# Queries turned ahead of a wait and copied out of PSUM by ScalarE instead of VectorE, in a four-layer kernel

## The chip, the cores and the metric

The kernel runs on one core of a Trainium2 chip. The metric is the device time of one execution in microseconds; the number compared is the median of several executions. Five engines take part, each with its own queue of instructions worked off in order, and they meet only in semaphores: TensorE (PE; matrix products and transposes into PSUM), VectorE (DVE), ScalarE (ACT), GpSimd (POOL) and SyncE (SP, which issues the transfers here). PEld is TensorE's weight load. PSUM holds eight banks of 512 f32 per partition.

## The reference, cut to what matters

Four residual layers are applied in turn to x of 8 x 16 x 16 x 64 f32, each on a group norm of x: a convolution, a memory layer, a local attention and a two-dimensional scan. The change lies in the end of the memory layer:

```python
q = _l2norm(jnp.einsum('btcd,de->btce', x, Wq))
def step(carry, x_t):          # 16 steps: one gradient step on each image's own weights
    ...
    new_mom = jax.tree.map(upd_m, mom, g)
    new_params = jax.tree.map(upd_p, params, new_mom)
(paramsT, momT), _ = jax.lax.scan(step, (params0, mom0), jnp.swapaxes(x, 0, 1))
final = jax.tree.map(lambda p: jnp.mean(p, axis=0), paramsT)
return _mlp(final, q)          # for w1, w2 in params: h = h + gelu(h @ w1) @ w2
```

Each of the 8 images has its own four matrices, called w10, w20 (first block of the small network) and w11, w21 (second block) in the kernel. After the 16 steps they are averaged over the images, and the averaged network is applied to the normalised queries q. The queries depend on x alone and not on the 16 steps.

## The kernel before

All of x stays on the chip. Each engine has its own program, written out by hand in one order; no planner moves anything. The memory layer projects keys, gates and queries, and GpSimd writes the normalised queries, positions in rows, into the buffer hf (L339, semaphore `q_spread`) before the loop of 16 steps (`Fori`) begins. The loop body spreads over four engines. The last things a step does are: TensorE's outer products for the gradients (helper line L1110), w10's last (semaphore `g10`); GpSimd's decayed copies of the weights (L350, L359, semaphores `kept_...`); and VectorE's updates, which add the momentum in PSUM banks 0 to 3 to the decayed copy. These are w10 (L754), w20, w11 and, at the head of the next step or behind the loop, w21 (all three at helper line L747). Each update sets the semaphore of its matrix (`w10_new` and so on), which reaches 17 with the last one.

Behind the loop the programs stand like this:

- TensorE waits for the last w10 and sums w10 over the images into bank 6 (`mean_of_images`, L1185, semaphore `wm_tp`). Then it waits for `q_spread`, turns the eight 128x128 blocks of hf into banks 4 and 5 (L1194, semaphore `q_tp` once, at the end), and waits for `wm_ready`, `qt_ready` and the last w11, w20 and w21. Then come the first up projection (`up`, L1204), the mean of w11 (L1185 again), and the down projection (`down`, L1211).
- ScalarE waits for `wm_tp`, evicts the mean as w10m (L514, `wm_ready`), and then applies gelu to the four banks of the up projection (L518).
- VectorE does the three remaining updates, waits for `q_tp`, copies both banks of turned queries at once into qt (L801, `qt_ready`), and then sums w20 and w21 over the images (L804 to L809, `wm_sum`), which the down projections take as weights. Later it adds qt to the first block's output (L811).
- GpSimd has nothing to do there until the layer's end.

Before the turned queries, banks 4 and 5 hold scratch of a step. Its last readers are ScalarE's and VectorE's operations that the last gradients wait for.

Of the kernel before, what the change touches and what calls it, by code (L numbers as in the profile page):

```python
# [10 lines left out]
ACT = mybir.ActivationFunctionType  # L11
# [4 lines left out]
BH, J = 2, 4  # L16
HW = H * W
POS = J * HW
NT = 2 * POS
P = 128  # L20
# [6 lines left out]
BANK = 512  # L27
# [50 lines left out]
def conv_attn_scan_kernel(nc, xs_d, band_d, const_d, param_d, out_d):  # L78
    ctx = ExitStack()
    with ctx:  # L80
        def sb(name, shape):
            return ctx.enter_context(nc.sbuf_tensor(name, shape, F32))
# [3 lines left out]
        def sem(name):  # L86
            if name not in sems:
                sems[name] = ctx.enter_context(nc.semaphore(name))
            return sems[name]

        ps = ctx.enter_context(nc.psum_tensor("ps", [P, 8, BANK], F32))
        psf = ps[:, :, :].rearrange("p b n -> p (b n)")
# [4 lines left out]
        def cst(name, rows=P):  # L97
            a, b = CONST_COLS[name]
            return const[0:rows, a:b]

        def par(name):
            a, b = PARAM_COLS[name]
            return param[:, a:b]

        ident = cst("ident")
# [51 lines left out]
        qt = sb("qt", [P, POS])  # L157
# [47 lines left out]
        hf = sb("hf", [P, POS])  # L205
# [204 lines left out]
        def _(act):  # L410
# [99 lines left out]
                               ACT.Copy).then_inc(sem("x_now"), 1)  # L510


            act.wait_ge(sem("wm_tp"), 1)
            act.activation(w10m[:, :], ps[:, 6, 0:E1], ACT.Copy, scale=1.0 / B).then_inc(sem("wm_ready"), 1)  # L514
            for i in range(2):
# [92 lines left out]
        def _(dve):  # L608
# [134 lines left out]
            def updated(m, new, grad, count):  # L743

                dve.wait_ge(sem(grad), count)
                dve.wait_ge(sem("kept_" + new), count)
                dve.tensor_tensor(by_pair(w11 if m == 1 else we[:, m, :]), momentum(m), by_pair(qe[:, m, :]), ALU.add)\  # L747
                   .then_inc(sem(new), 1)
# [47 lines left out]
                updated(1, "w11_new", "g11", t + 1)  # L796

            updated(2, "w21_new", "g21", NS + 1)

            dve.wait_ge(sem("q_tp"), 1)  # L800
            dve.tensor_copy(qt[:, :], psf[:, 4 * BANK:6 * BANK]).then_inc(sem("qt_ready"), 1)  # L801

            dve.wait_ge(sem("w20_new"), NS + 1)
            link(dve.tensor_reduce(wms[:, 0, :], we[:, 0, :].rearrange("p (b d) -> p d b", b=8), AX_X, ALU.add))  # L804
# [158 lines left out]
        def _(pe):  # L963
# [18 lines left out]
            for q in range(2):  # L982
                mm = pe.matmul(ps[:, 1, :], inv512[:, :], sq[:, q, :], start=(q == 0), stop=(q == 1))
# [14 lines left out]
            for d in range(3):  # L998
                pe.matmul(ps[:, 1, :], bandv[96:128, d, 2, :], xpad[96:128, 0, :, d:d + C], start=(d == 0), stop=False)
                mm = pe.matmul(ps[:, 0, :], bandv[0:32, d, 2, :], xpad[0:32, 1, :, d:d + C], start=False, stop=(d == 2))  # L1000
# [4 lines left out]
            for m in range(2):  # L1005
                mm = pe.matmul(ps[:, 2, 0:2], cst("sum16"), csum[:, :, m], start=(m == 0), stop=(m == 1))
# [4 lines left out]
            for q in range(2):  # L1011
                pe.wait_ge(sem("x1_rows"), q + 1)
                for j in range(J):
                    col = 2 * BANK + j * HW + q * P
                    mm = pe.transpose(psf[:, col:col + P], xs[:, q, j * P:(j + 1) * P], ident)
# [25 lines left out]
            for hh in range(2):  # L1041
                for j in range(J):
                    if hh == 0:
                        pe.wait_ge(sem("xn_ready"), j + 1)
                    at = (hh * J + j) * 2 * P
                    mm = pe.matmul(psf[:, at:at + P + 6], xn[:, j * HW + hh * P:j * HW + hh * P + P], keys_gates, start=True, stop=True)
                mm.then_inc(sem("kg_done"), 1)
            for hh in range(2):
                for j in range(J):
                    mm = pe.matmul(ps[:, 4 + hh, j * P:(j + 1) * P], xn[:, j * HW + hh * P:j * HW + hh * P + P], par("wq"), start=True, stop=True)  # L1050
# [18 lines left out]
            for bank in range(J):  # L1069
                mm = pe.matmul(ps[:, bank, :], zero_bf[:, 0:P], zero_bf[:, :], start=True, stop=True)  # L1070
# [6 lines left out]
            with pe.Fori(0, NS) as t:  # L1077
# [21 lines left out]
                def turn(bank, col, x):  # L1099
                    return pe.transpose(ps[:, bank, col:col + P], x, ident)  # L1100
# [47 lines left out]
                for n, x in enumerate((act_u[:, 0, :], h1bd, rbd, k_now)):  # L1148
                    mm = turn(7, n * P, x[:, :])
# [15 lines left out]
                for j in range(J):  # L1165
                    mm = pe.matmul(ps[32 * j:32 * j + 32, 5, 3 * P:4 * P], dhbd[:, 32 * j:32 * j + 32], wd[:, 0, P * j:P * j + P],  # L1166
                                   start=True, stop=True)
# [10 lines left out]
                gradient(3, k_lr, dz0_tok).then_inc(sem("g10"), 1)  # L1178


            pe.wait_ge(sem("w10_new"), NS + 1)

            def mean_of_images(w):
# [3 lines left out]

            mean_of_images(w10).then_inc(sem("wm_tp"), 1)

            pe.wait_ge(sem("q_spread"), 1)  # L1190
            for hh in range(2):
                for j in range(J):
                    at = 4 * BANK + j * HW + hh * P
                    mm = pe.transpose(psf[:, at:at + P], hf[:, (hh * J + j) * P:(hh * J + j + 1) * P], ident)  # L1194
            mm.then_inc(sem("q_tp"), 1)
            pe.wait_ge(sem("wm_ready"), 1)
            pe.wait_ge(sem("qt_ready"), 1)

            def up(w, src, i):
                for n in range(4):  # L1200
# [36 lines left out]
            for n in range(NK):  # L1237
# [3 lines left out]
                for half in range(2):  # L1241
                    for i in range(J):
                        mm = pe.matmul(psf[32 * i:32 * i + 32, 2 * BANK + n * P:2 * BANK + (n + 1) * P],
                                       cst("head_sum")[:, 32 * half:32 * half + 32], prod[n % 4][:, (2 * i + half) * P:(2 * i + half + 1) * P],
                                       start=(half == 0), stop=(half == 1))
                mm.then_inc(sem("qk_sum"), 1)

            def turn_probs(slot, src):
                return pe.transpose(psf[:, 6 * BANK + slot * P:6 * BANK + (slot + 1) * P], src, ident)

            keep_warm(6, 7)
            for half, (first, end) in enumerate(EXP_PARTS):
                pe.wait_ge(sem("exp_done"), half + 1)
                for n in range(first, min(end, 8)):
                    mm = turn_probs(n, ex[:, n * P:(n + 1) * P])
# [199 lines left out]
```

## Time and profile before

| what | value |
|---|---|
| time, median of 3 runs | 324.86 us (324.80 to 325.09) |
| the profiled execution's own time | 322.84 us |
| its span, first to last instruction | 321.0 us |
| mean granted TensorE clock | 0.979 |
| TensorE busy | 280.7 us, 87% |
| VectorE busy | 212.1 us, 66% |
| GpSimd busy | 145.6 us, 45% |
| ScalarE busy | 144.6 us, 45% |

The profile is one execution, recorded by the hardware. Times in rows are microseconds from the start of the span, unless marked ns. A row of the timeline merges neighbouring instructions of one engine and line; in brackets stands how long the engine idled before it and what it waited for. The chain of waits is followed back from the last instruction to what released it each time; "issue" in it is time in which the engine waited for nothing that the profile shows. The loop of 16 steps lies between about 51 and 213 us, each step taking about 10.05 us; the attention and the scan follow behind about 234 us.

### The profile page before, as it was taken

The page shows a single profiled execution, that of the slowest core. Times are in us where ns is not written, and L with a number is a line of the kernel's source. Part 1 is how long each engine was busy: PE and PEld are TensorE (multiplying, and loading weights), DVE is VectorE, ACT ScalarE, POOL GpSimd, SP SyncE. Part 2 cuts the span into 40 slices and gives each one's busy share as a digit, 9 for nine tenths or more (in the row PEclk, how much of TensorE's full clock was granted, in tenths as well). Part 3 has the DMA queues.
Part 4 walks back from the last instruction along what each step waited for, and adds up shares of the span by engine and source line. Part 5 has one row for each costly group of instructions (what it writes and reads, how often), then busy time and mean ns, then how long its engine had stood idle before and what let it go on. Part 6 is the DMA issues. An engine that isn't in the chain of part 4 may idle for free.

```text
span 321.0 us, 8491 instructions
## 1 busy us (share of the span) xinstructions
PE 280.7 (87%) x3338; PEld 186.9 (58%) x3345; DVE 212.1 (66%) x392; ACT 144.6 (45%) x353; POOL 145.6 (45%) x227
## 2 busy tenths in 40 slices
PE   8698759999999999999999999979985774899992
PEld 3233545777777777777777777754333552446642
DVE  0827554656666566665666656675478699899995
ACT  2003554466454664546655466523311662078511
POOL 8300087776667766677666776650000067200000
PEclk9999977999999999999999999999999998999998
DMA  7000000000000000000000000000000000000001
GB/s 289 14 0 2 0 1 2 0 0 0 0 0 0 0 0 0 0 0 0 0 0 0 0 0 0 0 2 2 0 0 2 0 2 0 1 2 0 0 0 65
DMA packets 874, 3.09 MB, mean 10 GB/s; under 512 B 96, under 2 KB 96, under 8 KB 864
## 3 DMA queue, kind: packets, MB, share of 16 engines
q1 hardware_dynamic: 864, 2.96, 2.5%
q8 instruction: 6, 0.10, 0.1%
q14 instruction: 4, 0.03, 0.0%
HBM read 2.44 MB, written 0.52 MB: 9 GB/s over the span
## 4 chain that ended last, share of the span: by engine, by line
PE 68%; DVE 23%; ACT 3%; issue 3%; POOL 2%; DVEq 0%; POOLq 0%
PE ps L1100 16%; PE ps L1082 9%; PE ps L1091 9%; PE ps L1110 6%; DVE arena_mem L754 4%; PE ps L1287 3%; PE ps L968 3%; PE ps L1318 2%; DVE arena_att L830 2%; PE ps L1166 2%; PE ps L993 2%; PE ps L1211 2%; DVE uf L850 1%; PE ps L1326 1%; ACT act_u L471 1%
## 5 line engine op out<-in xcount | busy, mean ns | idle before, releaser
L968 PE MATMUL ps<-zero 128*128 128x512 bf16 x130 | 34.7, 412 | 5.2 <-DVE uf L850 2.9
L350 POOL TENSOR_TENSOR arena_mem<-arena_mem,keep_e 128x512 f32<-128x512 f32 x32 | 33.4, 1043 | 0.0
L359 POOL TENSOR_TENSOR arena_mem<-arena_mem,keep_d 128x512 f32<-128x512 f32 x32 | 33.3, 1040 | 0.0
L747 DVE TENSOR_TENSOR arena_mem<-ps,arena_mem 128x512 f32<-128x512 f32 x49 | 32.0, 681 | 0.0
L481 ACT ACTIVATE arena_mem<-ps 128x512 f32<-128x512 f32 x48 | 28.7, 597 | 7.1 <-PE ps L1100 5.0
L1100 PE MATMUL ps<-const_sb,arena_mem 128*128 128x128 f32 x192 | 31.5, 287 | 0.0
L968 PEld LDWEIGHTS ps<-zero 128*128 128x128 bf16 x137 | 13.6, 106 | 24.6 <-issue 9.2
L471 ACT ACTIVATE act_u<-ps 128x128 f32<-128x128 f32 x32 | 8.9, 277 | 38.1 <-PE ps L1082 38.1
L366 POOL TENSOR_SCALAR z_e<-z_sq 128x128 f32<-128x128 f32 x32 | 9.5, 298 | 33.4 <-ACT z_sq L472 33.3
L1091 PE MATMUL ps<-act_u,arena_mem 128*64 128x16 f32 x512 | 20.6, 211 | 2.3
L1091 PEld LDWEIGHTS ps<-act_u,arena_mem 128*64 128x64 f32 x512 | 18.0, 137 | 7.7 <-issue 6.6
L765 DVE TENSOR_TENSOR ps<-ps,eta_d 128x512 f32<-128x512 f32 x32 | 22.1, 691 | 0.0
L765 DVE TENSOR_TENSOR ps<-ps,eta_e 128x512 f32<-128x512 f32 x32 | 22.1, 691 | 0.0
L1100 PEld LDWEIGHTS ps<-const_sb,arena_mem 128*128 128x128 f32 x192 | 20.1, 140 | 1.5
L770 DVE SCALAR_TENSOR_TENSOR z_y<-z_sq,ps 128x128 f32<-128x128 f32 x32 | 9.2, 288 | 16.9 <-ACT z_sq L472 16.3
L754 DVE TENSOR_TENSOR arena_mem<-ps,arena_mem 128x512 f32<-128x512 f32 x16 | 11.1, 692 | 13.2 <-PE ps L1110 13.2
L1110 PE MATMUL ps<-arena_mem 32*128 32x128 f32 x512 | 18.8, 283 | 0.2
L399 POOL TENSOR_TENSOR arena_att<-arena_att 128x1024 f32<-128x1024 f32 x2 | 5.5, 2761 | 28.7 <-DVE arena_att L850 28.6
L1110 PEld LDWEIGHTS ps<-arena_mem 32*128 32x128 f32 x512 | 15.8, 186 | 4.4 <-issue 4.4
L499 ACT ACTIVATE arena_mem<-ps,lrn 128x512 f32<-128x512 f32 x16 | 11.0, 687 | 10.8 <-PE ps L1100 10.8
L369 POOL TENSOR_TENSOR z_f<-z_e,act_u 128x128 f32<-128x128 f32 x32 | 14.6, 456 | 2.7
L791 DVE SCALAR_TENSOR_TENSOR arena_mem<-arena_mem,ps 128x128 f32<-128x128 f32 x16 | 4.6, 288 | 16.3 <-PE ps L1166 16.3
(267 smaller groups left out, 634.0 us busy)
## 6 DMA issues: line engine op xcount, KB each, us to landing
param_sb<-param SPq DMA_DIRECT2D x1, 840.5 KB, 7.2
arena_conv<-band SPq DMA_DIRECT2D x1, 576.0 KB, 5.6
xs_sb<-xs SPq DMA_DIRECT2D x1, 512.0 KB, 3.2
out<-xh SPq DMA_DIRECT2D x2, 256.0 KB, 2.1
const_sb<-const SPq DMA_DIRECT2D x1, 449.5 KB, 4.1
```

The costliest lines, as they stand in the source:

```text
L350: pool.tensor_tensor(qe[:, m, :].rearrange("p (b d) -> p b d", b=8), we[:, m, :].rearrange("p (b d) -> p b d", b=8), keep_e[:, bass.ts(t, ...
L359: pool.tensor_tensor(by_pair(kept), by_pair(w), keep_d[:, bass.ts(t, J)].unsqueeze(2).broadcast_to([P, J, E1]), ALU.mult).then_inc(sem("ke ...
L369: pool.tensor_tensor(z_f[:, i, :], z_e[:, i, :], act_u[:, i, :], ALU.mult).then_inc(sem("pool_link"), 1)
L481: act.activation(we[:, 1, :] if m == 1 else wd[:, m, :], ps[:, bank, :], ACT.Copy, scale=scale).then_inc(sem(cp), 1)
L747: dve.tensor_tensor(by_pair(w11 if m == 1 else we[:, m, :]), momentum(m), by_pair(qe[:, m, :]), ALU.add)\
L754: dve.tensor_tensor(by_pair(w10), momentum(3), by_pair(q10), ALU.add).then_inc(sem("w10_new"), 1)
L765: dve.tensor_tensor(v, v, eta, ALU.mult).then_inc(sem("scaled"), 1)
L968: pe.matmul(ps[:, bank, :], zero_bf[:, 0:P], zero_bf[:, :], start=True, stop=True)
L1082: mm = pe.matmul(ps[64 * h:64 * h + 64, bank, col + 32 * j:col + 32 * j + 32], w[:, P * j + 64 * h:P * j + 64 * h + 64], x[:, 32 * j:32 * ...
L1091: mm = pe.matmul(ps[64 * g:64 * g + 64, bank, col + n:col + n + W], w[:, P * j + 64 * g:P * j + 64 * g + 64], x[:, n:n + W], start=False, ...
L1100: return pe.transpose(ps[:, bank, col:col + P], x, ident)
L1110: mm = pe.matmul(ps[:, j, P * m:P * m + P], left[32 * j:32 * j + 32, :], right[32 * j:32 * j + 32, :], start=False, stop=False, skip_group ...
```

## The change

TensorE turns the queries before it waits for the last w10, not after the mean. The order of the eight blocks changes, so that bank 4 is complete after four of them and bank 5 after eight; `q_tp` is set once for each bank. ScalarE copies each bank into its half of qt, one instruction each, ahead of the eviction of w10m, and sets `qt_ready` twice; VectorE's copy of both banks is gone. The projection waits for both halves. What is computed is the same.

```diff
@@ scalar, behind the loop
+            for hh in range(2):
+                act.wait_ge(sem("q_tp"), hh + 1)
+                act.activation(qt[:, hh * BANK:(hh + 1) * BANK], ps[:, 4 + hh, :], ACT.Copy).then_inc(sem("qt_ready"), 1)
             act.wait_ge(sem("wm_tp"), 1)
             act.activation(w10m[:, :], ps[:, 6, 0:E1], ACT.Copy, scale=1.0 / B).then_inc(sem("wm_ready"), 1)
@@ vector, behind the loop
             updated(2, "w21_new", "g21", NS + 1)
 
-            dve.wait_ge(sem("q_tp"), 1)
-            dve.tensor_copy(qt[:, :], psf[:, 4 * BANK:6 * BANK]).then_inc(sem("qt_ready"), 1)
-
@@ tensor, behind the loop
+            pe.wait_ge(sem("q_spread"), 1)
+            for j in range(J):
+                for hh in range(2):
+                    at = 4 * BANK + j * HW + hh * P
+                    mm = pe.transpose(psf[:, at:at + P], hf[:, (hh * J + j) * P:(hh * J + j + 1) * P], ident)
+                if j % 2:
+                    mm.then_inc(sem("q_tp"), 1)
             pe.wait_ge(sem("w10_new"), NS + 1)
...
             mean_of_images(w10).then_inc(sem("wm_tp"), 1)
 
-            pe.wait_ge(sem("q_spread"), 1)
-            for hh in range(2):
-                for j in range(J):
-                    at = 4 * BANK + j * HW + hh * P
-                    mm = pe.transpose(psf[:, at:at + P], hf[:, (hh * J + j) * P:(hh * J + j + 1) * P], ident)
-            mm.then_inc(sem("q_tp"), 1)
             pe.wait_ge(sem("wm_ready"), 1)
-            pe.wait_ge(sem("qt_ready"), 1)
+            pe.wait_ge(sem("qt_ready"), 2)
```

## Rows read from the trace of the kernel before

**Rows 1.** The page's busy table: busy us, share of the span, instructions.

```profile
PE 280.7 (87%) x3338; PEld 186.9 (58%) x3345; DVE 212.1 (66%) x392; ACT 144.6 (45%) x353; POOL 145.6 (45%) x227
```

**Rows 2.** The chain of waits from 210 us: start, length, engine, line.

```profile
210.87 1.21 PE ps L1110 x32
212.11 0.70 DVE arena_mem L754
212.81 0.04 issue
212.85 1.16 PE ps L1185 x8
214.01 0.89 PE ps L1194 x8
214.92 1.24 DVE qt L801
216.16 0.09 issue
216.25 1.99 PE ps L1204 x8
218.24 1.09 PE ps L1185 x8
219.33 1.99 PE ps L1211 x8
```

**Rows 3.** Timeline before, inside and behind the loop: start, length, engine, line, operation.

```profile
52.88 1.90 POOL L339 TENSOR_TENSOR hf<-qraw,q_inv 128x1024 f32<-128x1024 f32 x1
...
200.83 1.17 PE L1110 MATMUL ps<-arena_mem 32*128 32x128 f32 x32
201.93 0.30 PEld L1097 LDWEIGHTS ps<-k_now,const_sb 128*128 128x128 f32 x2
...
211.88 1.04 POOL L350 TENSOR_TENSOR arena_mem<-arena_mem,keep_e 128x512 f32<-128x512 f32 x1
212.72 1.87 DVE L747 TENSOR_TENSOR arena_mem<-ps,arena_mem 128x512 f32<-128x512 f32 x3
212.85 1.16 PE L1185 MATMUL ps<-arena_mem,const_sb 128*128 128x128 f32 x8 [0.81 <-DVE arena_mem L754]
213.74 0.91 PEld L1194 LDWEIGHTS ps<-const_sb,hf 128*128 128x128 f32 x8
213.85 1.04 PE L1194 MATMUL ps<-const_sb,hf 128*128 128x128 f32 x8
214.05 0.28 ACT L514 ACTIVATE w10m<-ps 128x128 f32<-128x128 f32 x1 [2.80 <-PE ps L1185]
217.12 0.20 DVE L805 TENSOR_SCALAR wme<-wms 128x64 f32<-128x64 f32 x1
```

**Rows 4.** Single lines, L1194 and L481: count, shortest/median/longest ns, first and last start.

```profile
L1194 PE MATMUL ps<-const_sb,hf x8: 272/272/273, 213.8 to 214.6; 128*128 128x128 f32 x8
L481 ACT ACTIVATE arena_mem<-ps x48: 597/597/599, 54.3 to 207.8; 128x512 f32<-128x512 f32 x48
```

**Rows 5.** Windows: length, busy us (instructions) by engine, granted clock, DMA share, GB/s.

```profile
40.00:50.00 10.00, 6.55 (x32) 4.12 (x32) 5.56 (x14) 5.11 (x11) 7.00 (x8) 0.74 0.00 1
50.00:60.00 10.00, 9.86 (x137) 7.03 (x135) 4.18 (x9) 4.94 (x15) 9.12 (x12) 0.91 0.01 2
...
214.00:216.20 2.20, 0.89 (x9) 0.65 (x6) 1.87 (x3) 0.28 (x1) 0.00 (x0) 1.00 0.00 0
...
270.00:271.00 1.00, 0.00 (x0) 0.13 (x2) 0.97 (x2) 0.00 (x0) 1.00 (x1) 0.58 0.00 0
...
273.00:274.00 1.00, 1.00 (x4) 0.35 (x3) 0.97 (x2) 0.00 (x0) 0.00 (x0) 0.71 0.00 0
```

**Rows 6.** Timeline of TensorE near the end of the attention.

```profile
271.02 4.67 PE L968 MATMUL ps<-zero 128*128 128x512 bf16 x15 [2.90 <-DVE uf L850]
```

**Rows 7.** The chain of waits where the scan layer begins.

```profile
279.52 0.93 PE ps L1276 x8
```

## The prediction

> **What bounds the kernel now.** I read the page's busy table first, then the chain of waits around the edited lines, then the timeline of the same stretch engine by engine, and last the clock by windows. TensorE is busy 87% of the span [rows 1], but that share says nothing about this edit, which lies in a stretch of some 4 us just behind the sixteen-step loop. There the chain [rows 2] shows one thread: the last gradients on TensorE (L1110), the w10 update on VectorE (L754), the mean of w10 (L1185), the eight query transposes (L1194), the copy of the queries (L801), the first up projection (L1204). All later steps hang from that projection. Three pieces of the thread are the edit's: 0.89 us of transposes, 1.24 us of copy, 0.09 us until the projection starts, at 216.25.
>
> The reader is to see that the copy is late for two reasons. The transposes stand behind the mean, though their input, hf, was written by GpSimd at 52.88 to 54.78 [rows 3]. And they are read by VectorE, which until 214.59 (212.72 + 1.87) is busy with the three other weight updates. TensorE meanwhile idles 0.81 us waiting for w10, and ScalarE idles 2.80 us, from 211.25, before its one small eviction [rows 3].
>
> **The change part by part.**
>
> *Transposes moved ahead of the w10 wait.* Eight instructions, no DMA. Their pitch is (1.04 - 0.272) / 7 = 0.110 us, and the first load leads the first transpose by 0.11 us [rows 3, 4]. They can follow the last gradient directly. In the loop the instruction behind L1110 loads its weights 1.10 us after L1110 begins (200.83 to 201.93), so here the first load is expected at 210.87 + 1.10 = 211.97 [rows 3]. Four transposes (bank 4) are then done at 211.97 + 0.11 + 0.272 + 3 x 0.110 = 212.68, eight at 213.12. The eight pitches free TensorE for the mean at about 211.97 + 0.88 = 212.85, which is when w10 arrives anyway (212.81 + 0.04) [rows 2]. So the transposes lie in the idle 0.81 us and cost nothing, or up to 0.1 us if a pitch is lost; the mean ends at 214.01 to 214.11. If that cover were gone (TensorE starting its first instruction behind the loop only at 212.85, the latest time that the trace allows), the whole 0.89 us would stand ahead of the mean.
>
> *Copy on ScalarE in two halves.* Evictions of 128x512 f32 from PSUM by the same operation took 597 ns, 48 times [rows 4]. The first runs from 212.72 to 213.32, the second, its bank long ready, to 213.92. Queued behind these two new waits is the eviction of w10m, 0.28 us, and behind it the gelus. The mean ends after both copies, so w10m is evicted at 214.15 to 214.43 and nothing is delayed. The split also lets ScalarE read bank 4 while TensorE writes bank 5. In all ScalarE spends 1.19 us where VectorE spent 1.23; it is the place, not the rate, that counts.
>
> *Copy taken off VectorE.* VectorE goes from its last update at 214.59 straight to the two reductions that stood behind the copy. They feed the down projection by way of L805. That result came at 217.32 and was wanted at 219.33 [rows 2, 3]; with everything 1.5 to 1.6 us earlier the slack of 2.0 us stays. No gain and no loss.
>
> *What is late next.* The projection waits for w10m (ready for use at 214.43 + 0.09 = 214.52), for both copies (213.92), and, as before, for w21. That update is the third of the L747 group and ends at 214.59; GpSimd's part of it was there at 212.92 [rows 3]. This is the new last wait. The step from VectorE's end to the projection was 0.09 us with the copy, and 0.04 us from the w10 update to the mean [rows 2]. So the projection starts between 214.63 and 214.68; I take 214.67, nearer to the row of the same instruction. Gain: 216.25 - 214.67 = 1.58 us, from 1.57 to 1.62.
>
> *The rest.* From the projection to the end, the chain runs through TensorE, VectorE and ScalarE with no anchor to the old copy, so I let all of it move rigidly. The up projection, second mean and down projection follow each other with no gap [rows 2].
>
> **A rule weighed.** What the trace shows: the first TensorE instruction behind the loop began 0.04 us after its wait ended, and ScalarE's, L514, 0.04 us after the mean's end at 214.01 [rows 2, 3]; VectorE's third update, already behind its loop, ran on without a break. But TensorE was covered by 0.81 us and ScalarE by 2.80 us, and the edit uses up both covers. The Trainium skill, page "Runtime: NRT & Kernel Launch", section "Instruction fetch mechanics", says that code is fetched ahead in sequence and that a taken branch to code outside the held pages stalls the engine until it is fetched. By that rule the code behind a loop might not be there when the engine leaves it; no row here shows such a stall, nor excludes one under the cover. It is the first rival below, priced from rows.
>
> **The rivals.**
>
> *A. An engine is not ready right behind its loop.* TensorE at the latest: first load at 212.85, transposes done at 214.00, mean moved by 0.89 us to end at 214.90, w10m at 214.94 to 215.22, projection at 215.31: a gain of 0.94, 323.9. ScalarE at the latest: copies from 214.05 to 215.25, w10m to 215.53, projection at 215.62: a gain of 0.63, 324.2. For it: the covers hide what happened. Against: in the loop TensorE went from the last gradient to the next step's first load without any gap, and VectorE's third update had none. Chance 0.14, nearly all of it still faster.
>
> *B. The time is given back later.* Some consumer behind the projection is held by something that does not move. For it only that I assume rigidity over 100 us. Against: the slack of the wme sums is 2.0 us, and the other operands come out of this same chain. It would have to swallow at least 0.95 of the 1.58 us to leave no measurable change; I put it at 324.6. Chance 0.05.
>
> *C. The clock drops where TensorE leads.* TensorE's granted clock is at half, 1.2 of its 2.4 GHz, in a stretch that begins within 270:271 and ends within 273:274. That is within an idle time of TensorE from 268.12 to 271.02, and behind it, where VectorE is what TensorE waits for, so it costs little or nothing today [rows 5, 6]. An earlier one covers parts of 40:50 and 50:60, by the means 0.74 and 0.91 about 2 x (0.26 + 0.09) x 10 = 7 us [rows 5]. From 279.52 on TensorE leads [rows 7]. If the edit moved a drop there, each us of it at half would cost 0.5 us: a stretch of 3.4 us costs 1.7 and leaves 325.0; one of 7 us costs 3.5 and gives 326.8. It decides from about 3.2 us of low clock on the chain, and is measurably slower from 4.5 us. For it: a drop does lie some 6 us ahead of that stretch. Against: the spacing of later work is unchanged, the idle time of TensorE ahead of the projection shrinks (from 214.89 to 216.25 before, 1.36 us; about 0.6 after), and the clock is 1.00 in 214.00:216.20 [rows 3, 5]. Chance 0.05, 0.04 of it slower and 0.01 no change.
>
> *D. The copy was not what the projection waited for.* A wait is put down to whatever came last, so w21 or w10m might be it. The times exclude a large part of this: w21 was written at 214.59 and w10m at 214.33, the copy ended at 216.15 [rows 2, 3]. Should the projection wait for something that the trace does not show, nothing would change: 324.9. Chance 0.02.
>
> **How the numbers follow.** The sum is made on the profiled execution, 322.84 us with its span of 321.0: it becomes 321.26 with a span of 319.4. The median of the runs shown, 324.86, is 2.02 us above that execution; I keep that offset: 324.86 - 1.58 = 323.28, predicted 323.3. Chances: forecast 0.74, A 0.14, B 0.05, C 0.05, D 0.02. The three runs lie within 0.29 us of each other, and about 0.2% (0.65 us) is what a measurement of this kernel can tell from no change. The forecast's own range is 322.9 to 323.6. The range 322.7 to 324.3 takes in A's two ends as well and leaves out B, C, D and what of the forecast the runs scatter away. Faster: 0.74 of the forecast and 0.13 of A, 0.87. No change: 0.01 of A, 0.05 of B, 0.01 of C and 0.02 of D, 0.09. Slower: 0.04 from C.
>
> **What would show it right or wrong.** In the changed kernel's timeline: the first transpose load near 211.97 behind the last gradients (near 212.85 means A on TensorE); ScalarE's two copies of about 0.60 us ending near 213.9 (starting at 214 means A on ScalarE); the mean starting within 0.1 us of w10's end; no VectorE copy between the third update and the reductions; the projection within 0.1 us of that update's end, with w21's update named as its releaser. The distance from the start of the first projection to the end of the span should remain 104.8 us (321.0 - 216.25); longer means B or C, and the clock by windows behind 279 tells which. The prediction is wrong if the projection starts after 215.6, or if that distance grows by over 0.5 us.

## The result and the profile after

The changed kernel takes 322.64 us (median of 9 executions, 322.13 to 323.61) against 324.86 us (median of 9, 322.47 to 325.68) for the kernel before on the same chip. The ratio is 0.9943, interval 0.9918 to 0.9968: between 1.0 and 2.7 us less. A second series of the changed kernel gave 0.9924 (0.9891 to 0.9957). The comparisons leave out executions in which TensorE's clock stayed low for far longer; the profiles of two runs below, "One up product ahead of that wait" and "The changed kernel again", are of such executions.

The two profiled executions don't show that directly: 322.84 us and a span of 321.0 before, 323.33 us and a span of 321.5 after. The gain is in the stretch that was changed, and something ahead of it covers it up. The chain of waits after, from the last gradients on; compare [rows 2]:

```profile
212.85 1.21 PE ps L1110 x32
...
215.29 1.29 DVE arena_mem L750 x2
216.58 0.14 issue
216.72 1.99 PE ps L1205 x8
```

Transposes and copy have left the chain. It now goes through VectorE's updates to the first up projection (L1205), 3.87 us behind the start of the last gradients, where it was 216.25 - 210.87 = 5.38 us [rows 2]: 1.51 us less. From there to the end of the span it is 321.53 - 216.72 = 104.81 us, where it was 104.79. The timeline of the same stretch, beside [rows 3]:

```profile
213.95 0.86 PEld L1185 LDWEIGHTS ps<-const_sb,hf 128*128 128x128 f32 x8
214.65 1.08 ACT L515 ACTIVATE qt<-ps 128x512 f32<-128x512 f32 x2 [1.42 <-PE ps L1185]
214.69 1.88 DVE L750 TENSOR_TENSOR arena_mem<-ps,arena_mem 128x512 f32<-128x512 f32 x3
214.88 1.11 PE L1192 MATMUL ps<-arena_mem,const_sb 128*128 128x128 f32 x8
216.03 0.28 ACT L517 ACTIVATE w10m<-ps 128x128 f32<-128x128 f32 x1 [0.30 <-PE ps L1192]
216.72 1.99 PE L1205 MATMUL ps<-qt,w10m 64*128 64x512 f32 x8 [0.72 <-DVE arena_mem L750]
218.64 1.16 PE L1192 MATMUL ps<-arena_mem,const_sb 128*128 128x128 f32 x8
```

The transposes' first load comes 1.10 us behind the start of the last gradients, both copies are done at 215.73, w10m at 216.31, and the projection's idle time ends with VectorE's L750, the updates.

Why then is the span longer? The last gradients start at 212.85 in place of 210.87, though nothing was changed ahead of them. The clock by windows of the changed kernel (length, busy time of PE, PEld, DVE, ACT, POOL, granted clock), and TensorE's timeline in the first two steps:

```profile
56.00:58.00 2.00, 0.55 (x4) 0.37 (x6) 0.87 (x3) 0.00 (x0) 1.64 (x6) 0.94 0.00 0
58.00:60.00 2.00, 2.00 (x24) 1.63 (x28) 0.92 (x2) 0.43 (x2) 2.00 (x3) 0.50 0.00 0
...
64.00:66.00 2.00, 1.85 (x35) 1.51 (x33) 1.31 (x3) 0.55 (x3) 0.48 (x2) 0.86 0.00 0
```

```profile
57.45 0.55 PE L1097 MATMUL ps<-rbd,const_sb 128*128 128x128 f32 x2 [2.59 <-DVE z_p L784]
...
60.53 2.09 PE L1110 MATMUL ps<-arena_mem 32*128 32x128 f32 x32
72.15 1.17 PE L1110 MATMUL ps<-arena_mem 32*128 32x128 f32 x32
```

The same two groups of gradients in the kernel before:

```profile
60.19 1.17 PE L1110 MATMUL ps<-arena_mem 32*128 32x128 f32 x32
70.23 1.17 PE L1110 MATMUL ps<-arena_mem 32*128 32x128 f32 x32
```

TensorE was granted half its clock (0.50) in the loop's first two steps, from 57.7 to 64.6 us, right behind an idle time of 2.59 us. From the first step's gradients to the second's it took 11.62 us, against 10.04 before, and from there on the two profiles stay 1.9 to 2.0 us apart. In the profile before, the low stretch lay just ahead of the loop and reached into its beginning [rows 5]. The profiled execution before was also a quick one, 2.0 us below its median, and the one after lies 0.7 us above its own. So a single pair of profiles misleads here, and the edit has to be read from its own stretch. The numbers below are taken so: from the start of the last gradient group to the first up projection ("the stretch": 5.38 before, 3.87 after) and from there to the end ("the rest": 104.8).

### The profile page after: what moved, and what is told of

It is laid out like the page before. It is cut to its first block, busy times and chain, and to the rows that moved or that the text cites. A ratio compares the mean times of both kernels' runs of the same rounds, so it can differ in the third digit from the quotient of the medians.

```text
span 321.5 us, 8492 instructions
## 1 busy us (share of the span) xinstructions
PE 280.4 (87%) x3338; PEld 189.0 (59%) x3345; DVE 210.7 (66%) x391; ACT 145.8 (45%) x355; POOL 145.8 (45%) x227
## 4 chain that ended last, share of the span: by engine, by line
PE 66%; DVE 22%; issue 4%; ACT 3%; POOL 3%; POOLq 0%; DVEq 0%
PE ps L1100 15%; PE ps L1082 9%; PE ps L1091 9%; PE ps L1110 6%; DVE arena_mem L757 3%; PE ps L1288 3%; PE ps L1319 2%; PE ps L968 2%; PE ps L1166 2%; PE ps L1055 2%; DVE arena_att L830 2%; PE ps L993 2%; PE ps L1212 2%; PE ps L1097 1%; PE ps L1327 1%
## 5 line engine op out<-in xcount | busy, mean ns | idle before, releaser
L968 PE MATMUL ps<-zero 128*128 128x512 bf16 x130 | 32.5, 393 | 6.3 <-DVE uf L850 2.7
L750 DVE TENSOR_TENSOR arena_mem<-ps,arena_mem 128x512 f32<-128x512 f32 x49 | 32.0, 681 | 0.0
L481 ACT ACTIVATE arena_mem<-ps 128x512 f32<-128x512 f32 x48 | 28.7, 597 | 7.1 <-PE ps L1100 4.9
L471 ACT ACTIVATE act_u<-ps 128x128 f32<-128x128 f32 x32 | 8.9, 277 | 37.2 <-PE ps L1082 37.2
L1110 PE MATMUL ps<-arena_mem 32*128 32x128 f32 x512 | 19.7, 292 | 0.1
L1110 PEld LDWEIGHTS ps<-arena_mem 32*128 32x128 f32 x512 | 16.6, 194 | 4.5 <-issue 4.5
```

What stands on the lines that cost most here:

```text
L481: act.activation(we[:, 1, :] if m == 1 else wd[:, m, :], ps[:, bank, :], ACT.Copy, scale=scale).then_inc(sem(cp), 1)
L1110: mm = pe.matmul(ps[:, j, P * m:P * m + P], left[32 * j:32 * j + 32, :], right[32 * j:32 * j + 32, :], start=False, stop=False, skip_group ...
```

## The experiments

**Transposes early, VectorE's copy kept.**

```diff
-            for hh in range(2):   # scalar
-                act.wait_ge(sem("q_tp"), hh + 1)
-                act.activation(qt[:, hh * BANK:(hh + 1) * BANK], ps[:, 4 + hh, :], ACT.Copy).then_inc(sem("qt_ready"), 1)
+            dve.wait_ge(sem("q_tp"), 2)   # vector, behind updated(2, ...)
+            dve.tensor_copy(qt[:, :], psf[:, 4 * BANK:6 * BANK]).then_inc(sem("qt_ready"), 1)
```

> Transposes early as in the change, but VectorE copies both banks behind its last update as before. Measured from the start of the last gradient group to the start of the first up projection (5.38 us before, 3.87 us in the changed kernel). Theory (the copy's place on VectorE is the larger part; the transposes alone only take away VectorE's 0.33 us wait): the copy starts at +3.73, takes 1.23, projection at about 5.05, so 0.3 us gained of 1.5. Rival (the 0.89 us of transposes on the chain are a gain of their own): projection at about 4.5. Whole time: theory about 0.3 us below before, rival 0.9 us below.

The timeline, from the last gradients to the projection:

```profile
213.80 1.17 PE L1110 MATMUL ps<-arena_mem 32*128 32x128 f32 x32
215.65 1.88 DVE L747 TENSOR_TENSOR arena_mem<-ps,arena_mem 128x512 f32<-128x512 f32 x3
217.44 1.22 DVE L801 COPY qt<-ps 128x1024 f32<-128x1024 f32 x1
218.76 1.99 PE L1205 MATMUL ps<-qt,w10m 64*128 64x512 f32 x8 [1.81 <-DVE qt L801]
```

The stretch is 4.96 us: 0.42 gained, nearer to the theory's 0.3 than to the rival's 0.9. The copy stands behind the updates with no idle time ahead of it. The whole time can't be told from before: 0.9988 (0.9963 to 1.0013).

**ScalarE's copies, transposes left behind the mean.**

```diff
+            act.wait_ge(sem("wm_tp"), 1)   # w10m first, then the two copies
+            act.activation(w10m[:, :], ps[:, 6, 0:E1], ACT.Copy, scale=1.0 / B).then_inc(sem("wm_ready"), 1)
             for hh in range(2):
                 act.wait_ge(sem("q_tp"), hh + 1)
...
             mean_of_images(w10).then_inc(sem("wm_tp"), 1)   # tensor: the eight transposes follow here
+            pe.wait_ge(sem("q_spread"), 1)
```

> Transposes behind the mean as before, ScalarE copies bank by bank behind the eviction of w10m. From the start of the last gradient group to the first up projection. Theory: transposes end at about +4.0, the first copy starts at +3.6, the second ends at about +4.7 and the projection starts at 4.8, so 0.6 us gained of 1.5; with the other half done alone 0.3, the two halves together give more than their sum because each alone leaves the other on the chain. Rival (the engine that copies is all that counts): 3.9, the whole gain.

```profile
211.92 1.17 PE L1110 MATMUL ps<-arena_mem 32*128 32x128 f32 x32
215.53 1.08 ACT L517 ACTIVATE qt<-ps 128x512 f32<-128x512 f32 x2 [0.16 <-PE ps L1194]
216.72 1.99 PE L1205 MATMUL ps<-qt,w10m 64*128 64x512 f32 x8 [0.78 <-ACT qt L517]
```

The stretch is 4.80, as the theory had it: 0.58 gained, 0.9967 (0.9936 to 0.9998) in the whole time. Alone, the two halves of the edit give 0.42 and 0.58 us, together 1.51. Each alone leaves the other's work on the chain.

**One copy of both banks by ScalarE.**

```diff
+            act.wait_ge(sem("q_tp"), 2)
+            act.activation(qt[:, :], psf[:, 4 * BANK:6 * BANK], ACT.Copy).then_inc(sem("qt_ready"), 1)
```

> The changed kernel with one copy of both banks by ScalarE behind all eight transposes. Theory (the last update of w21 is the new last wait, and copies and w10m lie under it): the copy takes 1.02 us from about +2.2 to +3.2, w10m follows the mean as in the changed kernel or at most 0.15 us later, projection at 3.87 within 0.1 us. Rival (the split by banks is part of the gain): projection 0.3 to 0.6 us later.

```profile
212.78 1.17 PE L1109 MATMUL ps<-arena_mem 32*128 32x128 f32 x32
215.01 1.02 ACT L514 ACTIVATE qt<-ps 128x1024 f32<-128x1024 f32 x1 [1.86 <-PE ps L1184]
216.64 1.99 PE L1204 MATMUL ps<-qt,w10m 64*128 64x512 f32 x8 [0.73 <-DVE arena_mem L749]
```

3.86 us in its one execution: the split by banks gains nothing here. The one copy ends 3.25 us behind the start of the last gradients, the two ended 2.88 us behind it, and the updates, which the projection waits for, end at 3.72 in either kernel.

**One up product ahead of that wait.**

```diff
-UP_BANKS = ((0, 1, 3, 7), (0, 1, 2, 3))
+UP_BANKS = ((7, 0, 1, 3), (0, 1, 2, 3))
...
                     if i:
                         pe.wait_ge(sem("uf_ready"), 4 * i)
+                    elif n == 1:
+                        pe.wait_ge(sem("w11_new"), NS + 1)   # and w20_new, w21_new
```

> The changed kernel with the first of four up products put into bank 7, which no update reads, ahead of the waits for the last w11, w20 and w21; the other three behind them. Theory (VectorE's last update is the last wait, w10m was there 0.4 us earlier): the first up product starts about 0.3 us earlier, at +3.5 to +3.6, the others follow without a gap, and the end of the span comes 0.3 us earlier: time 0.3 us (0.1%) below the changed kernel, 0.7% below before. Rival (w10m or an overhead of the projection itself is the limit): no change of the projection's start.

The timeline: VectorE's updates; of TensorE the product's first pass by itself, the two passes after it, all eight passes, and the second mean. The row by itself shows the first two passes in the changed kernel, which begin together.

```profile
218.13 1.17 PE L1110 MATMUL ps<-arena_mem 32*128 32x128 f32 x32
219.97 1.88 DVE L750 TENSOR_TENSOR arena_mem<-ps,arena_mem 128x512 f32<-128x512 f32 x3
221.63 0.69 PE L1209 MATMUL ps<-qt,w10m 64*128 64x512 f32 x1 [0.37 <-ACT w10m L517]
222.00 0.76 PE L1209 MATMUL ps<-qt,w10m 64*128 64x512 f32 x2
...
221.63 2.35 PE L1209 MATMUL ps<-qt,w10m 64*128 64x512 f32 x8 [0.37 <-ACT w10m L517]
...
223.91 1.16 PE L1192 MATMUL ps<-arena_mem,const_sb 128*128 128x128 f32 x8
```

```profile
216.72 0.71 PE L1205 MATMUL ps<-qt,w10m 64*128 64x512 f32 x2 [0.72 <-DVE arena_mem L750]
```

The first half of the expectation held: the product starts at +3.50, when w10m is there. The second half fell: the products take 2.35 us in place of 1.99, and the second mean starts at +5.78, as in the changed kernel (218.64 - 212.85 = 5.79). So by the trace nothing is gained; the ratio, 0.991 (0.9878 to 0.9941), does not tell it apart from the changed kernel. The clock was full throughout (1.00 from 218 to 225 us). In the changed kernel the eight passes start in four pairs, the two of a pair 0.01 to 0.04 us apart, at 216.72, 217.22, 217.65 and 218.08. Here they form two rows of four, each with about the same spacing: one from 221.63, the other only from 222.00, 0.15 us behind the end of the updates (219.97 + 1.88 = 221.85). So two passes run at a time, and the second row came 0.37 us late. The products use 64 rows each, two the lower and two the upper ones; as I read it, the two of the lower rows were now alone until the first of the upper rows was let go. Which pass belongs to which product the trace doesn't name. The run with all four products ahead tests that.

**The changed kernel again.** No edit.

> The changed kernel once more, beside the next ones. Theory (the edit's gain is 1.5 us between the last gradients and the first up projection; the longer span of the first profile comes from where TensorE's low clock fell, 57.7 to 64.6 us, inside the first loop steps): the stretch from the start of the last gradient group to the first up projection is 3.87 us within 0.05, from there to the end of the span 104.8 us, while the time ahead of it differs from the first profile by up to 2 us with the place of the low clock. Rival (the change itself makes the part ahead of the loop's end longer): the last gradient group again starts near 212.85 wherever the low clock lies. Time about 1.5 us below before.

```profile
218.30 1.17 PE L1110 MATMUL ps<-arena_mem 32*128 32x128 f32 x32
222.16 1.14 PE L1205 MATMUL ps<-qt,w10m 64*128 64x512 f32 x4 [0.73 <-DVE arena_mem L750]
```

```profile
60.00:70.00 10.00, 10.00 (x111) 7.39 (x110) 4.57 (x9) 3.18 (x11) 3.75 (x7) 0.50 0.00 0
70.00:80.00 10.00, 9.81 (x119) 7.88 (x119) 3.24 (x7) 3.28 (x11) 5.05 (x7) 0.58 0.00 0
```

The stretch is 3.86 us again. The last gradients start 5.4 us later than in the first profile of the same kernel, with the clock at half through most of 60 to 80 us: more than the 2 us that the theory allowed, but the rival, a fixed 212.85, fell. The low clock began at 58 us as in the first profile; what differs is that it lasted three times as long. The rest is 106.15, not 104.8; the run "The kernel before again" shows why.

**All four up products ahead of that wait.**

```diff
-UP_BANKS = ((0, 1, 3, 7), (0, 1, 2, 3))
+UP_BANKS = ((7, 4, 5, 6), (0, 1, 2, 3))
...
+            up(w10m, qt, 0)
             pe.wait_ge(sem("w11_new"), NS + 1)
             pe.wait_ge(sem("w20_new"), NS + 1)
             pe.wait_ge(sem("w21_new"), NS + 1)
-            up(w10m, qt, 0)
-            mean_of_images(w11).then_inc(sem("wm_tp"), 1)
+            mean_of_images(w11, 2).then_inc(sem("wm_tp"), 1)
...
-            down(wme[:, 0, :], 4, 0)
+            down(wme[:, 0, :], 0, 0)
```

> The changed kernel with all four first up products in banks 7, 4, 5 and 6, which no weight update reads, ahead of the waits for w11, w20 and w21 (the down projection's result moves to banks 0 and 1, the mean of w11 to bank 2). Theory (the one product put ahead in the run before gained nothing because its partner of the other row half started only behind w21, and the two halves run side by side): the products start at +3.50 behind the last gradient group and take 1.99 us again, the second mean starts 0.36 us earlier than in the changed kernel (+5.43 in place of +5.79), and the rest follows: 0.36 us less. Rival (the products or the second mean are held by something else): second mean at +5.79 again.

```profile
211.89 1.17 PE L1110 MATMUL ps<-arena_mem 32*128 32x128 f32 x32
215.39 1.99 PE L1205 MATMUL ps<-qt,w10m 64*128 64x512 f32 x8 [0.37 <-ACT w10m L517]
217.32 1.16 PE L1192 MATMUL ps<-arena_mem,const_sb 128*128 128x128 f32 x8
```

Products at +3.50, 1.99 us again, second mean at +5.43: the theory to the hundredth. The rest is 104.86, so 0.32 us of the 0.37 reach the end. The projection now waits for ScalarE's w10m. In whole time 0.9928 (0.99 to 0.9956); 0.3 us on top of the changed kernel is not to be seen there.

**The normalisation of the queries left out.** GpSimd's power and multiplication ahead of its loop are dropped.

```diff
-            inverse_norm(q_inv[:, :], q_ss[:, :], 3, 16).then_inc(sem("q_inv"), 1)
-            pool.wait_ge(sem("q_inv"), 1)
-            pool.tensor_tensor(hf[:, :]...)   # qraw times q_inv, q_spread
```

> The changed kernel without the queries' normalisation on GpSimd ahead of its loop (no q_inv, no multiplication; the squares of the queries are turned in place of the normalised ones). It leaves 4.8 us of GpSimd's work out at 49 to 54 us. Theory (that work holds up the first step's slope factors, TensorE idles 2.6 us for it, and the low clock of some profiles begins right behind that idle time): no idle time of 2.6 us in the first step, no low clock beginning between 56 and 62 us, the first w10 gradients 2 to 3.5 us earlier, the whole time 2.5 us or more below the changed kernel. Rival (the low clock comes at that place whatever TensorE did before): a low stretch begins there again and the gain is 2 us or less. The stretch behind the loop stays at 3.87 us by both.

TensorE's timeline at the last gradients and the windows in which the changed kernel's clock was at half:

```profile
206.83 1.17 PE L1105 MATMUL ps<-arena_mem 32*128 32x128 f32 x32
```

```profile
54.00:56.00 2.00, 2.00 (x32) 1.36 (x30) 1.20 (x2) 1.48 (x4) 2.00 (x3) 1.00 0.00 0
56.00:58.00 2.00, 1.91 (x39) 1.30 (x35) 0.94 (x3) 0.49 (x3) 2.00 (x3) 1.00 0.00 0
58.00:60.00 2.00, 1.76 (x35) 1.43 (x36) 1.96 (x5) 0.54 (x3) 0.64 (x3) 1.00 0.00 0
```

TensorE works through 54 to 58 us, the clock stays full, and the last gradients start at 206.83, 6.0 us earlier than in the changed kernel's first profile and 4.0 earlier than before [rows 2]. The first step's gradients come 4.4 us earlier than there (56.11 against 60.53), more than the 2 to 3.5 expected; 0.7 us of that was there already at 45 us. The stretch is 3.86 us, as expected. Median 318.78 us, ratio to before 0.9827 (0.9778 to 0.9877). So the normalisation of the queries costs more at the head of the loop than their transposes and copy did at its end: it holds GpSimd when the first step wants it. How much of the 4.4 us is the wait and how much the low clock behind it, this run doesn't separate.

**The kernel before again.** No edit.

> The kernel before once more. Theory (the place of the low clock differs from run to run of one kernel): from the last gradient group to the first up projection 5.38 us within 0.05, from there to the end 104.8 us, and the start of the last gradient group anywhere from 210.5 to 213 us according to where the low clock lies. Rival (the low clock's place belongs to the kernel): 210.87 within 0.3 us and a low stretch at 44.9 to 51.7 us again.

```profile
210.59 1.17 PE L1110 MATMUL ps<-arena_mem 32*128 32x128 f32 x32
215.97 1.56 PE L1204 MATMUL ps<-qt,w10m 64*128 64x512 f32 x6 [1.36 <-DVE qt L801]
```

```profile
252.00:254.00 2.00, 1.65 (x10) 1.42 (x11) 0.00 (x0) 1.86 (x3) 0.00 (x0) 0.84 0.00 0
254.00:256.00 2.00, 2.00 (x12) 2.00 (x11) 1.23 (x1) 1.02 (x1) 0.00 (x0) 0.50 0.00 0
```

The stretch is 5.38 again. As to the place of the low clock this run leans to the rival: last gradients at 210.59, and a mean clock of 0.57 in 44 to 52 us, the same as in the first profile. But the rest is 321.90 - 215.97 = 105.93, not 104.8. The low clock of 253.4 to 256.8 lies on the attention's turned weights. There the chain holds, where the first profile had 1.11 us of TensorE and then VectorE:

```profile
253.00 3.38 PE ps L1055 x16
256.41 1.23 DVE arena_att L850
257.63 2.14 DVE arena_att L863
```

L863 begins 41.66 us behind the projection, 1.10 later than in the first profile (256.81 - 216.25 = 40.56). A low clock there cost 1.1 us. Behind 270 us it cost next to nothing: it lasted 6.8 us here and 3.4 us in the first profile, and the rests differ by 1.14 (105.93 - 104.79), hardly more than those 1.10. The other profiles agree: in the five (this one among them) with a low stretch that begins 37.2 to 37.6 us behind the projection's start, the rest is 105.8 to 106.2; in five others it is 104.8 to 104.9; and in the run with one product ahead 105.1, of which 0.36 are its longer products. The executions of this kernel that were compared had spans from 320.8 to 325.2 us, so the two traces are not the whole of it.

In both profiles of this kernel TensorE has no such idle time in the first step (busy 9.86 of the 10 us from 50 to 60 [rows 5]), and the clock is full there. Over all eleven profiles: in the seven where TensorE idled 1.04 to 2.60 us at that place, the half clock began 0.1 to 1.8 us behind the idle time; in the other four the clock was full from 52 to 66 us. With the normalisation in one piece, the idle time was shorter or absent where the clock had already been at half just ahead of the loop, from 45 to 48 us on. Why the clock fell there in some profiles and not in others no run shows, and whether the edit changes where and how often it falls stays open.

**The normalisation cut into the steps.** Added to the kernel with all four products ahead; the reference is computed in full.

```diff
             with pool.Fori(0, NS) as t:
+                pool.tensor_tensor(q_inv[:, bass.ds(t, 1)], q_ss[:, bass.ds(t, 1)], cst("minus_half"), ALU.pow).then_inc(sem("q_inv"), 1)
+                pool.wait_ge(sem("q_inv"), t + 1)
+                pool.tensor_tensor(hf[:, bass.ts(t, C)], qraw[:, bass.ts(t, C)], q_inv[:, bass.ds(t, 1)].broadcast_to([P, C]),
+                                   ALU.mult).then_inc(sem("q_spread"), 1)
...
-            pe.wait_ge(sem("q_spread"), 1)
+            pe.wait_ge(sem("q_spread"), NS)
```

> The kernel with all first up products ahead of w21, and the queries' normalisation cut into 16 pieces, one at the head of each loop step on GpSimd (one column of the power and a 128x64 product), where GpSimd waits 1.1 us or more in the traces; what is computed is the whole reference again. Theory (the normalisation in one piece held up the first step, and the low clock behind it came from TensorE's 2.6 us of idle time there): each piece takes 0.6 to 0.9 us, steps stay at 10.05 us, the first step has no idle time of 2 us, no low clock begins between 50 and 62 us, and the time is near that of the run without the normalisation, 319 to 320 us, 3 us or more below the changed kernel. Rival (the pieces push GpSimd's slope factors later in every step): steps grow by 0.3 us or more, 16 x 0.3 = 5 us lost again, time at 323 us or above. The stretch behind the loop by both: first up product at +3.50.

GpSimd's timeline at the head of the second step, then two neighbouring gradient groups and the first up products:

```profile
61.50 0.56 POOL L344 TENSOR_TENSOR q_inv<-q_ss,const_sb 128x1 f32 x1
62.35 0.29 POOL L347 TENSOR_TENSOR hf<-qraw,q_inv  x1 [0.29 <-POOL q_inv L344]
62.83 0.30 POOL L370 TENSOR_SCALAR z_e<-z_sq 128x128 f32<-128x128 f32 x1 [0.18 <-ACT z_sq L476]
...
69.55 1.17 PE L1114 MATMUL ps<-arena_mem 32*128 32x128 f32 x32
79.61 1.17 PE L1114 MATMUL ps<-arena_mem 32*128 32x128 f32 x32
...
213.76 1.99 PE L1209 MATMUL ps<-qt,w10m 64*128 64x512 f32 x8 [0.37 <-ACT w10m L521]
```

The pieces fit: GpSimd still waits 0.18 us for the step's squares, and the steps stay at 10.05 to 10.06 us. The stretch is 3.51 us, as expected. Median 321.15 us (318.79 to 322.98), ratio to before 0.989 (0.985 to 0.993): clearly faster than before. By its ratio it is also faster than the kernel that it was added to (0.9928, 0.99 to 0.9956), but the two intervals overlap, and the 319 to 320 us expected were not reached. In the profile the first step has no such idle time and the clock is full from 50 to 60 us, but it was low in 46 to 50 us, ahead of the loop, and again at the attention's beginning, with a rest of 105.78. Three other profiles with a low clock as short as this one ahead of the loop still had 1.04 to 1.34 us of idle time and a drop behind it. So, by this one profile, the version took away the drop behind the idle time that it removed, and not the others.

## Why the prediction was right, and where it was off

- *Transposes in TensorE's idle time*: right. First load 1.10 us behind the last gradients, as worked out; the mean starts at +2.03, between +1.98 and +2.08.
- *Two copies on ScalarE*: right, and a little quicker. They take 1.08 us together, not 1.19, from +1.80; w10m is evicted from +3.18, 0.1 earlier than worked out. The run with one copy shows that the split, which I took as given, was of no use.
- *w21 as the next wait*: right. The trace names the updates, and putting the four products ahead of them gained the further 0.37 us of the stretch that this leaves.
- *The projection's start*: 0.07 us off. I took 0.08 us from the update's end to the projection; it is 0.15 (216.57 to 216.72). That is the whole difference between 1.58 worked out and 1.51 measured; why this step is longer than the 0.09 us behind the copy, no run shows.
- *The rest moves rigidly*: right for the work (104.81 against 104.79), and wrong as a forecast of any one execution. With the clock low at the attention's beginning the rest is 105.8 to 106.2, in the kernel before as in others.
- *Rival A, an engine not ready behind its loop*: did not occur. The transposes followed the last gradients without a gap and ScalarE started as soon as the first bank was turned; the rule of the Trainium skill that was weighed with it has no stall to explain here. *Rival D* fell too: the projection came earlier once the copy was out of its way. *Rival B*: nothing is given back behind the stretch.
- *Rival C*: I looked for the costly drop behind 279 us. The traces show it elsewhere: in the changed kernel's first loop steps, and at the attention's beginning in the kernel before (253 us) as well as in the changed one (259 us). The idea that a drop costs where TensorE leads holds; the place was wrong. Taking the profile's own span forward by the sum, 321.0 to 319.4, missed because of the 2.0 us lost in the first steps: it came out at 321.5.
- *The whole time*: the median of 322.64 is 0.6 us below the forecast of 323.3 and just under its range, 322.7 to 324.3. The medians differ by 2.2 us and the changed stretch by 1.5; for the 0.7 us between them no trace shows a cause, and the two profiled executions even differ the other way. The interval, 1.0 to 2.7 us, holds the sum. So it is the stretch that bears the mechanism out; the whole time alone would not have told this sum from one half a microsecond smaller or larger.
- *The noise*: I read 0.29 us of scatter from three executions. Nine of the same kernel span 3.2 us, and the intervals are near 0.25% to each side. A gain of 0.5% is told apart from none; the two halves of the edit, 0.13% and 0.18%, are hardly so.

## What to carry to other kernels

When an input has long been ready, let the engine that will wait anyway prepare it ahead of its wait, and let an engine that idles there move it on; do both, since either alone leaves the other on the path. Then look for the next wait by its end time: here one update, which ended 0.3 us behind the eviction of w10m, took over. Where runs scatter by more than the edit, measure from one event of the trace to the next, and ask what sits ahead of an idle time of TensorE: here it was the normalisation of the same queries, in one piece at the head of GpSimd's queue.

## What was not expected of the hardware

Two products of 64 rows each, on different row halves, run side by side on TensorE: their passes start in pairs 0.01 to 0.04 us apart, eight in 1.99 us. The Trainium skill, page "TensorE: Matmul & The Clock Gate", section "Part 3: Packing small matmuls — row/col tiling", says that products in different row groups of the array can run at the same time; the trace agrees. Holding back one of the halves by a semaphore made them 2.35 us and took back all that an earlier start had gained. And an idle time of 2.59 us on TensorE in the loop's first step was followed by half clock in the rest of that step and the next; with the work that caused it left out the clock stayed full there, and the last gradients came 4 to 6 us earlier, by the missing wait and the full clock together.
